# Queries and keys in 32-row tiles of TensorE, in place of zero-padded tiles per head

## The reference, cut to what matters

```python
qkv = x @ W_qkv.T                       # 128 -> 3 * 128, 16 heads of 8
s = (q @ k.T) / sqrt(8)                 # per batch and head: 1024 x 1024
s = s + mask                            # layer 1: |i - j| <= 32 (a band); layer 3: j <= i (causal)
out = softmax(s) @ v                    # then the output projection, a gate, the residual
```

## Time and profile before

| | us |
|---|---|
| median of three runs | 2231.25 (2226.29 to 2231.28) |
| the profiled execution | 2228.59 |
| its span, first to last instruction | 2226.8 |
| TensorE busy | 1930.5 |
| VectorE busy | 1543.7 |
| ScalarE busy | 1190.7 |
| GpSimd busy | 888.9 |

### The profile page before, as it was taken

One profiled execution on the slowest core, in us unless ns is written; L12 is line 12 of the kernel. 1 busy time (PEld: TensorE's weight loads), 2 busy tenths in 40 slices (PEclk: granted clock), 3 DMA queues, 4 the chain that ended last, 5 costly groups with the idle time before them and its releaser, 6 DMA issues. The chain is left out here.

```text
span 2226.8 us, 35726 instructions
## 1 busy us (share of the span) xinstructions
PE 1930.5 (87%) x13823; PEld 1497.2 (67%) x13823; DVE 1543.7 (69%) x3094; ACT 1190.7 (53%) x2340; POOL 888.9 (40%) x861
## 2 busy tenths in 40 slices
PE   5999999999999988988969888654797479999997
PEld 4888888888888876765757666532586345555554
DVE  5888888888888853356777677356665887777771
ACT  4667776676766744545745444313233335555544
POOL 3889998898989875021110000000266200000000
PEclk9999999999999998988989889667899679999999
DMA  2000000000000001000000000120154100000000
GB/s 74 13 1 13 1 13 13 1 13 1 1 1 1 1 1 48 1 18 10 20 0 2 1 1 2 38 62 0 33 141 93 28 1 1 1 1 1 1 1 20
DMA packets 50377, 37.50 MB, mean 17 GB/s; under 512 B 7496, under 2 KB 43624, under 8 KB 50208
## 3 DMA queue, kind: packets, MB, share of 16 engines
q1 hardware_dynamic: 43520, 30.49, 4.6%
q0 software_dynamic: 5632, 4.20, 1.4%
q10 hardware_dynamic: 1056, 0.52, 0.1%
HBM read 29.96 MB, written 5.24 MB: 16 GB/s over the span
## 5 line engine op out<-in xcount | busy, mean ns | idle before, releaser
L1723 ACT ACTIVATE ET_a<-PS 128x512 f32<-128x512 f32 (+1 forms) x512 | 252.4, 517 | 244.4 <-PE PS L1622 135.1
L661 POOL TENSOR_TENSOR dtl<-dts,dth 128x512 fp32r<-128x512 f32 x256 | 340.6, 1330 | 20.5
L593 DVE TENSOR_REDUCE nm<-PS 128x1 f32<-128x1024 f32 x256 | 311.5, 1217 | 20.3 <-PE PS L193 19.3
L659 POOL CAST dth<-dts 128x512 fp32r<-128x512 f32 x256 | 245.3, 958 | 67.3 <-ACT dts L526 67.3
L191 PE MATMUL PS<-xh,yh 128*128 128x512 f32 x512 | 224.8, 439 | 6.6 <-ACT G L519 4.2
L142 PE MATMUL PS<-C,XN 128*128 128x128 f32 x1120 | 178.7, 285 | 50.4 <-DVE XN L186 48.8
L192 PE MATMUL PS<-xl,yh 128*128 128x512 f32 x512 | 201.8, 394 | 0.0
L193 PE MATMUL PS<-xh,yl 128*128 128x512 f32 x512 | 201.6, 394 | 0.0
L519 ACT ACTIVATE XNT<-PS,nm 128x1024 f32<-128x1024 f32 x128 | 143.6, 1122 | 83.1 <-DVE nm L593 83.0
L519 ACT ACTIVATE G<-PS,nm 128x1024 f32<-128x1024 f32 x128 | 142.8, 1116 | 75.0 <-DVE nm L593 74.8
L142 PEld LDWEIGHTS PS<-C,XN 128*128 128x128 f32 x1120 | 139.8, 144 | 62.3 <-issue 36.8
(11 more groups left out here) (411 smaller groups left out, 5022.2 us busy)
## 6 DMA issues: line engine op xcount, KB each, us to landing
e_wg<-in_WgT SPq DMA_DIRECT2D x16, 256.0 KB, 2.8
e_wu<-in_WuT SPq DMA_DIRECT2D x16, 256.0 KB, 3.3
e_wd<-in_WdT SPq DMA_DIRECT2D x16, 256.0 KB, 3.8
wqn<-in_L_attn_Wq SPq DMA_DIRECT2D x8, 128.0 KB, 2.2
wkn<-in_L_attn_Wk SPq DMA_DIRECT2D x8, 128.0 KB, 2.5
wvn<-in_L_attn_Wv SPq DMA_DIRECT2D x8, 128.0 KB, 2.6
won<-in_WoT SPq DMA_DIRECT2D x8, 128.0 KB, 2.5
wvt<-in_WvT SPq DMA_DIRECT2D x8, 128.0 KB, 2.7
```

The lines of the kernel that those rows point to most:

```text
L593: e.tensor_reduce(self.nm[:, half, i:i + 1], self.S[half], AX.X, MAX, negate=True).then_inc(*self.top.up((g, half)))
L659: e.tensor_copy(hi, src).then_inc(*ts.up((g, g4, "h")))
L661: e.tensor_tensor(lo, src, f(hi), SUB).then_inc(*ts.up((g, g4, "l")))
L1723: e.activation(dst, src, ACT.Exp, scale=self.SC, bias=0.0).then_inc(*self.ex.up(it))
```

## The change

The padded tiles QH go. The queries get three tiles `QS`, written by the projection as the keys are, and a score matmul names 32 rows of QS and of KS and the place of those rows in the array. The mask matmuls stay as they are. The copies, the clears, their signals and their waits go; `maxima` becomes one instruction over 128 rows; the fence of the next stage waits for POOL's memset of XNT in place of POOL's last clear.

```diff
-        self.QH = [[sb(f"QH{n}_{i}", [128, 1024], F32R) for i in range(4)] for n in range(3)]
+        self.QS = [sb(f"QS{i}", [128, 1024], F32R) for i in range(3)]
...
 # pool: the clears of QH[2] are gone
-                e.tensor_copy(self.QH[2][i][:, 512 * c:512 * c + 512], self.scratch[:, 0:512]).then_inc(*self.clear_pool.up((i, c)))
...
 # row (col alike, with the operands exchanged, after a wait for ("max", n, 1))
-            s, ks, it = self.QH[n % 3][hh], self.KS[n % 3], ("row", x, j)
+            rows = slice(32 * hh, 32 * hh + 32)
+            s, ks, it, at = self.QS[n % 3][rows], self.KS[n % 3][rows], ("row", x, j), (32 * hh, 0)
             if j == 0:
-                q.wait_ge(self.q_act if hh % 2 == 0 else self.q_dve, ("q", n, 1, hh))
-                q.wait_ge(self.mi, ("project", n, 1, 1))
+                q.wait_ge(self.mi, ("project", n, 0, 1))
...
-                t = e.matmul(o[:, 0:wd], s[:, 128 * i:128 * i + 128], ks[:, c0:c0 + wd], start=True, stop=first)
+                t = e.matmul(o[:, 0:wd], s[:, 128 * i:128 * i + 128], ks[:, c0:c0 + wd], start=True, stop=first, tile_position=at)
                 if not first:
                     t = e.matmul(o[:, c1 - c0 - 128:c1 - c0], w.identb[:, :], w.mk[:, 0:128], start=False, stop=True)
...
 # act: the copies of heads 0 and 2 and the clears are gone
-                for hh in (0, 2):
...
-                    e.activation(self.QH[n % 3][hh][r, 512 * ck:512 * ck + 512], f(hn[r, :]), ACT.Copy).then_inc(*self.q_act.up(("q", n, ck, hh)))
...
 # dve, project
-            e.scalar_tensor_tensor(out=hn, in0=o, scalar=self.bq[:, w_, qd:qd + 1], in1=f(hn), op0=ADD, op1=SUB).then_inc(*self.mi.up(u))
...
-                e.tensor_copy(self.QH[n % 3][hh][r, cs], hn[r, :]).then_inc(*self.q_dve.up(("q", n, ck, hh)))
+            if n >= 3:
+                q.wait_ge(self.col, ("col", 4 * (n - 3) + 3, self.nc_ - 1))
+            dst = (self.QS if w_ == 0 else self.KS)[n % 3]
+            e.scalar_tensor_tensor(out=dst[:, cs], in0=o, scalar=self.bq[:, w_, qd:qd + 1], in1=f(hn), op0=ADD, op1=SUB).then_inc(*self.mi.up(u))
...
 # dve, maxima
-            for hh in range(4):
-                r = slice(32 * hh, 32 * hh + 32)
-                o = self.QH[n % 3][hh][r, 512 * c:512 * c + 512]
-                e.tensor_tensor(o, f(o), MI[r, :], ADD).then_inc(*self.mi.up(u + (hh,)))
+            o = self.QS[n % 3][:, 512 * c:512 * c + 512]
+            e.tensor_tensor(o, f(o), MI, ADD).then_inc(*self.mi.up(u))
```

More of the change, by code:

```diff
@@ L1448, in __init__ @@
         self.bank_last = last
-        mi, q_act, q_dve, ex, ao = [], [], [], [], []
+        mi = []
         def of(u):
             if u[0] == "project":
-                _, n, w_, ck = u
                 mi.append(u)
-                if w_ == 0:
-                    q_act.extend([("q", n, ck, 0), ("q", n, ck, 2)])
-                    q_dve.extend([("q", n, ck, 1), ("q", n, ck, 3)])
             elif u[0] == "max":
-                mi.extend([u + (h,) for h in range(4)])
+                mi.append(u)
             else:
@@ L1467, in __init__ @@
         self.mi = k.sig("a_side_done", mi)
-        self.q_act = k.sig("a_q_even", q_act)
-        self.q_dve = k.sig("a_q_odd", q_dve)
-        self.zero = k.sig("a_zero", ["scratch"])
         self.zero_m = k.sig("a_zero_max", ["m"])
-        self.clear_act = k.sig("a_clear_act", [(n, i) for n in (0, 1) for i in range(4)])
-        self.clear_dve = k.sig("a_clear_dve", [(n, i) for n in (0, 1) for i in range(4)])
-        self.clear_pool = k.sig("a_clear_pool", [(i, c) for i in range(4) for c in range(2)])
         self.row = k.sig("a_row", rows)
@@ L1484, in __init__ @@
         self.fin_d = k.sig("a_fin_sum", [(c, n) for c in range(4) for n in range(3 if kind == 3 else 2)])
-        self.ends = [(self.fin_p, 3), (self.fin_a, 3), (self.fin_d, self.fin_d.last), (self.clear_pool, (3, 1))]
+        self.ends = [(self.fin_p, 3), (self.fin_a, 3), (self.fin_d, self.fin_d.last), (self.zero_m, "m")]
         self.bq, self.bm = w.bq, w.bm
     def done_of(self, u):
-        return u if u[0] == "project" else u + (3,) if u[0] == "max" else u + (1,)
+        return u + (1,) if u[0] == "give" else u
     @staticmethod
@@ L1541, in pool @@
         e.memset(self.k.XNT[:, :], 0.0).then_inc(*self.zero_m.up("m"))
-        q.wait_ge(self.zero, "scratch")
-        for i in range(4):
-            for c in range(2):
-                e.tensor_copy(self.QH[2][i][:, 512 * c:512 * c + 512], self.scratch[:, 0:512]).then_inc(*self.clear_pool.up((i, c)))
     def pe(self, e, q):
@@ L1603, in row @@
                     oi = o[:, 256 * (i % 2):256 * (i % 2) + 256]
-                    e.matmul(oi, s[:, 128 * i:128 * i + 128], ks[:, r:r + 256], start=True, stop=False)
+                    e.matmul(oi, s[:, 128 * i:128 * i + 128], ks[:, r:r + 256], start=True, stop=False, tile_position=at)
                     u = r - 128 * i + 128
@@ L1610, in col @@
             n, hh, b, qd, h = self.head(x)
-            s, ks, it = self.QH[n % 3][hh], self.KS[n % 3], ("col", x, j)
+            rows = slice(32 * hh, 32 * hh + 32)
+            s, ks, it, at = self.QS[n % 3][rows], self.KS[n % 3][rows], ("col", x, j), (32 * hh, 0)
             if j == 0:
-                q.wait_ge(self.mi, ("max", n, 1, hh))
+                q.wait_ge(self.mi, ("max", n, 1))
             o = self.bank_free(q, it)
@@ L1619, in col @@
                 diag = q0 == 128 * jj
-                t = e.matmul(o[:, 0:wd], ks[:, 128 * jj:128 * jj + 128], s[:, q1 - wd:q1], start=True, stop=not diag)
+                t = e.matmul(o[:, 0:wd], ks[:, 128 * jj:128 * jj + 128], s[:, q1 - wd:q1], start=True, stop=not diag, tile_position=at)
                 if diag:
@@ L1626, in col @@
                     oi = o[:, 256 * (i % 2):256 * (i % 2) + 256]
-                    e.matmul(oi, ks[:, 128 * i:128 * i + 128], s[:, r:r + 256], start=True, stop=False)
+                    e.matmul(oi, ks[:, 128 * i:128 * i + 128], s[:, r:r + 256], start=True, stop=False, tile_position=at)
                     u = r - 128 * i + 128
@@ L1685, in act @@
         m3 = k.cst("m3")
-        def clear(n, c):
-            for i in range(4):
-                e.activation(self.QH[n][i][:, 512 * c:512 * c + 512], self.scratch[:, 0:512], ACT.Copy).then_inc(*self.clear_act.up((n, i)))
         def project(u, o):
@@ L1695, in project @@
             if self.hm_n[u] >= 2:
-                self.hm_free(q, self.first_and_side[self.hm_n[u] - 2])
+                q.wait_ge(self.mi, self.first_and_side[self.hm_n[u] - 2])
             q.wait_ge(w.ready, ("bm", 1))
@@ L1699, in project @@
             e.activation(hn, o, ACT.Identity, scale=m3[:, w_:w_ + 1], bias=self.bm[:, w_, qd:qd + 1]).then_inc(*self.mi_act.up(u))
-            if w_ == 0:
-                q.wait_ge(self.mi, u)
-                for hh in (0, 2):
-                    r = slice(32 * hh, 32 * hh + 32)
-                    self.q_free(q, n, hh)
-                    e.activation(self.QH[n % 3][hh][r, 512 * ck:512 * ck + 512], f(hn[r, :]), ACT.Copy).then_inc(*self.q_act.up(("q", n, ck, hh)))
         def col(x, j):
@@ L1711, in col @@
                 q.wait_ge(self.av, x - 2)
[L1712 to L1715, removed]
             q.wait_ge(self.col, it)
@@ L1729, in take_out @@
             e.activation(self.AVS[x // 2 % 2], k.bank(6), ACT.Copy).then_inc(*self.out.up(x))
-        q.wait_ge(self.zero, "scratch")
-        clear(0, 0)
         for n, u in enumerate(self.first):
@@ L1744, in act @@
                 late += 1
-            if x == 0 and j == 13:
-                clear(1, 1)
         for c in range(4):
@@ L1761, in hm_n @@
         return {u: n for n, u in enumerate(self.first_and_side)}
[L1763 to L1780, removed]
     def dve(self, e, q):
@@ L1785, in dve @@
         MI = k.bank(7)
-        def clear(n, c):
-            for i in range(4):
-                e.tensor_copy(self.QH[n][i][:, 512 * c:512 * c + 512], self.scratch[:, 0:512]).then_inc(*self.clear_dve.up((n, i)))
         def project(u, o):
@@ L1858, in row @@
                                 negate=True).then_inc(*self.top.up(it))
-        e.memset(self.scratch[:, 0:512], 0.0).then_inc(*self.zero.up("scratch"))
-        q.wait_ge(self.zero, "scratch")
-        clear(0, 1)
         for n, u in enumerate(self.first):
@@ L1872, in dve @@
                 late += 1
-            if x == 0 and j == 13:
-                clear(1, 0)
         for u in self.use:
```

## The result

The changed kernel takes 2800.07 us (median of four runs, 2795.88 to 2806.36) against 2231.27: a ratio of 1.256, interval 1.252 to 1.259. Slower was forecast, but not by a quarter: 569 us in place of 136.

The account below looks back on a forecast made before the run. TensorE was taken to bound both attentions. The profiled 2228.6 us plus 85 (layer 1) and 51 (layer 3) gave 2365, as a median 2367 us; 2315 to 2415 had chance 0.76, the 8-in-10 range was 2275 to 2420.

Parts of the forecast that it names:

- Price of a round trip: Score and mask pairs on TensorE: changing tile shape and back adds 0.28 us in layer 1, 0.23 in layer 3.
- Count and overlap: Steady heads: 16 round trips each in layer 1 (+116 us), 13.5 in layer 3 with four overlapping score pairs (+68 us).
- Maxima, copies, clears: Both attentions: fewer DVE additions, no query copies or clears; with 10 us of clock, saves 40 us in layer 1, 20 in layer 3.
- The start: Start of each attention: without copies and clears the first row score comes sooner, 5 us saved in each layer.
- The clock: TensorE's granted clock: pairs priced at full clock, with 10 us regained in layer 1 as stalls for DVE mostly go.
- the rival: Layer 1's clock falls: 512 pairs lose 0.37 us each, 190 us more, total 2557 us; chance 0.06.

Follow-up runs that it names:

- full_rows: Changed kernel without its tiles: each score matmul takes all 128 rows of QS and KS, summing over four heads; 2138.88 us, ratio 0.958.
- one_group32: Changed kernel with every score and mask in array rows 0 to 31; 2567.73 us, ratio 1.152 (a second run with rows 0 to 63: 2467.68 us, 1.105).
- full_witness: Changed kernel with 128-row scores without tiles, plus a 32-row matmul of 64 columns behind each mask; 2480.1 us, ratio 1.116.
- filler: Changed kernel with each mask added three times in layer 1 and five times in layer 3; 2983.52 us, ratio 1.338.
- rows64: Changed kernel with score tiles of 64 rows in place of 32, masks as they are; 2802.08 us, ratio 1.258.
- masks_first: Changed kernel reordered: at each step all masks first, then all 32-row scores, column and row in turn; 2382.2 us, ratio 1.067.

## Why the prediction was wrong

The steps, in its own order:

- *Price of a round trip*, 0.28 in layer 1: right at full clock (0.52 for 0.245). Layer 3 shows its price only in its first microseconds (0.32 and 0.16 us at 2011.15, as forecast). The one 8-row matmul of the earlier trace rows was a true witness for the fp32r tiles.
- *Count and overlap*: right. In the traces changes of shape rise from 122 to 1116 in layer 1 and from 558 to 1467 in layer 3, 31 and 28 a head (forecast about 31 and 27), and 110 neighbouring scores start together, the four a head that the count had.
- *Maxima, copies, clears*: right in sign, too small in size. 60 us forecast for both layers, 95 measured in full_rows. The start gave the 5 us per layer that it had (first projection to first score 10.05 to 5.05 us in layer 1, 9.94 to 5.05 in layer 3). In layer 1 the clock itself, 0.87 to 0.99, was part of it, priced at 10.
- *The clock* is the step that failed. The sum takes full clock for every pair: "Whether the wider spacing of the matmuls lets the clock stay up is the open point", and then prices the point at nothing and the rival at 0.06, for layer 1 alone. The reason given against it was that TensorE "would have work at nearly all times". It had: 531 of 540.8 us busy, and half clock. Busy in the profile says that an instruction is in the engine, not how many rows it fills or how long it waits to change shape. The argument also looked at the spacing only. What one_group32 shows is that small tiles bring layer 1's clock down with no spacing inside the pairs at all. In place of full clock the runs showed 0.59 and 0.51. With the savings 35 us larger than forecast and the other terms taken as forecast, the clock cost some 470 us (an estimate, 433 and 35).
- The rival let the clock fall, in layer 1 alone. It put 0.37 us on each pair for the half clock, 0.90 with the forecast's 0.53; measured are 0.83 for 0.52, 0.31 more. Its layer 1 would have been 275 us longer than before (85 + 190), against 242 measured and 85 forecast. What it lacked was layer 3, left out because its clock was 0.99 in the earlier trace rows; but it fell further: 0.51. Its pairs are the poorer in full work, a mask of 128 columns to a score of up to 512, which fits but isn't shown to be the reason. The trace of before held a hint: 0.66 in the part with rows alone, so layer 3 depended on the clock coming back. Of the 433 us beyond the forecast, 157 are layer 1's (241.7 for 85) and 275 layer 3's (326.1 for 51).

Open: in which measure rows, columns and gaps count together. one_group shows that rows count by themselves, full_rows against full_witness that gaps do (0.99 to 0.83 in layer 1). filler's layer 3 and rows64 show that adding some of one isn't always enough, and masks_first's layer 1 that few rows need not be harmful. Open too: whether layer 3 would keep its clock if it hadn't fallen at the start.

## What to carry to other kernels

Before scores or other matmuls are put into tiles of few rows, ask what then still fills the array. The zeros of the padded tiles cost TensorE no time here (a pair takes 0.245 us with them and without, in full_rows), and with them layer 3's steady part had 0.99 of the clock. A full matmul between tiles costs a round trip of 0.28 us at full clock. If tiles are wanted, put matmuls of one shape together and tiles of different row groups next to each other (layer 1: 265 us grouped, 541 ungrouped, 299 padded), and read the granted clock of the stage before the busy time. Take the parts of a change apart: here 92 us of savings lay under some 660 us of loss. And look whether the clock comes back after a pause, not only what it is on average.

## What the runs showed of the hardware

- A 32-row fp32r score of 256 columns is followed by its full mask 0.20 us later than its streaming takes, and the mask by the next score 0.10 us later, at full clock (1404.91). The forecast's split of the 0.20, half for the change and half for weights that aren't loaded ahead, fits but isn't shown by itself. At half clock the pair goes from 0.45 to 0.83.
- Layer 1, back-to-back pairs in 128, 64 and 32 rows: clock 0.99, 0.86, 0.59.
- Two 32-row score tiles of different row groups start within 0.01 us of each other (2305.66).
- Work added can shorten a stage by its clock: 541 to 512 us in layer 1 (0.59 to 0.94).
- TensorE can be busy without a break and stay at half clock: 761.2 of 761.2 us in the changed kernel's layer 3. After the fall at the stage's start the clock is back within 140 us in the five runs with full scores, and not until the last 20 us in the seven with tiled ones.
